# The last dense layer of a cross-attention block as seven block products, with y turned by VectorE and through DRAM

## The chip, the cores and the metric
One core of one Trainium2 chip runs the whole program. The metric is the device time of that core in microseconds. Before the change it is 2246.83 us, the median of 3 runs (2246.42 to 2249.33).

## What is computed
x and the context have 8 sequences of 256 rows and 1024 columns, in float32. The core of the reference, with the attention itself cut:

```python
x = x + attention(layernorm(x), ctx, ...)          # ends in a product with Wo, 4096 x 1024
y = layernorm(x)                                   # 2048 rows of 1024
zeros = qzeros[:, :, None] >> shifts & 15          # 4-bit zero points and weights in int32 words
w = qweight[:, None, :] >> shifts & 15             # 8 words' worth of rows: depth 1024
W = scales_full * (w - zeros_full)                 # 1024 x 1024, scales by groups of 128
x = x + y @ W + bias
```

The change touches the last two lines and the turning of y that they need. Products are made in a high and a low part of each operand: x = hi + lo, and three of the four partial products, high by high, high by low and low by high.

## The kernel before, in words
All five engines have programs written out by hand, with semaphores between them; nothing plans the order but the code. In the order of time: keys and values (to 0.16 of the span), 16 rounds of attention, the output projection (7 block products of 16 steps, numbers 0 to 111), and the last dense layer.

**The output projection** (`block_step`, lines 814 to 816) multiplies by blocks: halves of rows, of depth and of columns, in seven products instead of eight, of sums and differences of blocks. A step adds 24 matmuls of 128x512, three for each of the 8 banks of PSUM. For step s SyncE (SP) loads a left tile into `xring` and a right tile into `wraw` (`load_step`, lines 540 to 556), ScalarE makes the high parts (`step_hi`, lines 1027 and 1032), VectorE the left low part (`step_lo`, line 1339) and GpSimd the right low part (line 1634), before it a sum of right blocks (line 1646) where the product has one. `a_parts` and `b_parts` have two slots, so the parts of step s can be made when step s-2 is done. After a product VectorE adds its 8 banks to `rows` (`product_out`, line 1457); where a product goes to two places ScalarE copies it to `spare` and VectorE adds it again later (line 1464).

**The last dense layer before.** Ahead of it, within the projection's steps, VectorE unpacks the weights (`dense_full`, lines 1469 to 1474), ScalarE and VectorE make their high and low parts (lines 1101 and 1478), and from step 82 VectorE makes the statistics of the first 8 tiles of rows (line 1195) and normalizes four of them (`y_normalize`, line 1484). In the layer TensorE turns a tile of 128 rows by 8 transposes against the identity (`y_fill`, line 838), ScalarE and VectorE read the two banks as high and low part (lines 1132 and 1527), and TensorE makes two banks of 24 matmuls each (`products`, lines 241 to 243). VectorE adds each bank to its rows (line 1543), SP stores the tile (lines 603 and 607). The rest of the statistics and normalizations is done beside it; GpSimd adds the bias (line 1690). TensorE's work is 16 tiles x (8 transposes + 48 matmuls).

A part of the code as it stands, TensorE's order:

```python
for f in range(4):
    y_fill(f)
for r in range(16):
    dense(r)
    if r + 2 < 16:
        y_fill(2 * (r + 2))
        y_fill(2 * (r + 2) + 1)
```

## Time and profile before

| | us |
|---|---|
| median of 3 runs | 2246.83 (2246.42 to 2249.33) |
| span of the profiled execution | 2244.6 |
| TensorE busy | 2219.1 (99%) |
| VectorE busy | 1373.5 (61%) |
| GpSimd busy | 1392.6 (62%) |
| ScalarE busy | 1052.8 (47%) |
| granted clock of TensorE, mean | 1.000 |

The profiled execution's own time is given as its span, from the first to the last instruction; the time of a run contains also what lies around it, and the median is 2.2 us above the span. Busy time of TensorE counts overlapping matmuls once; a matmul's own 390 ns is longer than the distance between two of them, since they are pipelined. Idle time of an engine that isn't TensorE costs nothing here unless TensorE waits for it. The profile names the engines PE (TensorE), DVE (VectorE), ACT (ScalarE), POOL (GpSimd) and SP (SyncE), and L1339 is line 1339 of the kernel.

### The profile page before, as it was taken

Reading aid. Unit: us, or ns where it says so; the run is one execution under the profiler, and the core shown is the slowest. Engines: PE = TensorE matmul, PEld = TensorE weight load, DVE = VectorE, ACT = ScalarE, POOL = GpSimd, SP = SyncE. Lnnn points to the kernel's source line nnn. Section 1 sums busy time; section 2 is a strip of 40 time slices with the busy share of each in tenths; the row PEclk is TensorE's granted clock in tenths of the full one; section 3 lists DMA queues with packets and bytes.
Section 4 is the critical chain, followed back from the end, with each engine's and each line's share of the span. In section 5 each row is a group of like instructions: output and inputs, shape, how many; then the busy total and the mean of one; then the engine's idle time right before and its main releaser. Section 6 shows DMA issues by size and latency. Waiting matters only on the chain.

```text
span 2244.6 us, 33169 instructions
## 1 busy us (share of the span) xinstructions
PE 2219.1 (99%) x10562; PEld 1862.3 (83%) x10562; DVE 1373.5 (61%) x2536; ACT 1052.8 (47%) x2296; POOL 1392.6 (62%) x980
## 2 busy tenths in 40 slices
PE   8999999999999999999999999899999999999999
PEld 6888888888888888788888888778888888888887
DVE  4782575777777778877777777523675445453532
ACT  3232123767666767766666666622333333331100
POOL 1320453788888889888888888765663354454210
PEclk9999999999999999999999999999999999999999
DMA  6766675687888889887888888687654564451111
GB/s 248 269 230 217 237 269 200 204 255 242 242 260 237 245 251 271 252 262 237 242 249 248 241 250 243 205 320 259 199 187 151 162 197 151 158 193 69 47 47 47
DMA packets 299899, 476.71 MB, mean 212 GB/s; under 512 B 23568, under 2 KB 195888, under 8 KB 299824
## 3 DMA queue, kind: packets, MB, share of 16 engines
q1 hardware_dynamic: 285744, 440.12, 62.5%
q10 hardware_dynamic: 13312, 33.56, 3.8%
q0 software_dynamic: 768, 2.10, 0.3%
q8 instruction: 39, 0.64, 0.1%
q14 instruction: 36, 0.29, 0.0%
HBM read 303.70 MB, written 171.98 MB: 212 GB/s over the span
## 4 chain that ended last, share of the span: by engine, by line
PE 91%; DVE 3%; POOL 3%; DMA 1%; issue 1%; ACT 1%; SPq 0%; DVEq 0%; ACTq 0%; POOLq 0%
PE ps L241 22%; PE ps L242 22%; PE ps L243 22%; PE ps L814 9%; PE ps L815 8%; PE ps L816 8%; PE ps L838 1%; POOL rope_tmp L1561 1%; DMA left_scratch<-s_buf 0%; POOL s_buf L1561 0%; DVE rope_tmp L1170 0%; DVE rope_tmp L1171 0%; DVE rope_tmp L1169 0%; POOL wraw L1646 0%; ACT wq_t L882 0%
## 5 line engine op out<-in xcount | busy, mean ns | idle before, releaser
L241 PE MATMUL ps<-act_t,wq_t 128*128 128x512 f32 x1280 | 500.3, 391 | 1.3 <-DVE act_t L1232 0.6
L242 PE MATMUL ps<-act_t,wq_t 128*128 128x512 f32 x1280 | 499.6, 390 | 0.0
L243 PE MATMUL ps<-act_t,wq_t 128*128 128x512 f32 x1280 | 498.0, 389 | 0.0
L1634 POOL TENSOR_TENSOR b_parts<-wraw,b_parts 128x512 fp32r<-128x512 f32 x112 | 199.2, 1779 | 262.6 <-ACT b_parts L1032 262.6
L814 PE MATMUL ps<-b_parts,a_parts 128*128 128x512 f32 x896 | 349.1, 390 | 1.7 <-POOL b_parts L1634 1.4
L815 PE MATMUL ps<-b_parts,a_parts 128*128 128x512 f32 x896 | 348.6, 389 | 0.0
L816 PE MATMUL ps<-b_parts,a_parts 128*128 128x512 f32 x896 | 348.6, 389 | 0.0
L1339 DVE TENSOR_TENSOR a_parts<-xring,a_parts 128x1024 fp32r<-128x1024 f32 x112 | 147.7, 1318 | 303.7 <-ACT a_parts L1027 303.7
L1616 POOL TENSOR_TENSOR q_t<-pt_raw,q_t 128x1024 fp32r<-128x1024 f32 x124 | 302.5, 2440 | 46.3 <-ACT q_t L1010 43.5
L1561 POOL TENSOR_TENSOR rope_tmp<-rope_tmp 128x512 f32<-128x512 f32 x144 | 193.4, 1343 | 182.9 <-DVE rope_tmp L1171 182.8
L1027 ACT ACTIVATE a_parts<-xring 128x1024 fp32r<-128x1024 f32 x112 | 118.7, 1060 | 389.6 <-PE ps L816 385.5
L243 PEld LDWEIGHTS ps<-act_t,wq_t 128*128 128x128 f32 x1280 | 240.3, 188 | 51.0
L241 PEld LDWEIGHTS ps<-act_t,wq_t 128*128 128x128 f32 x1280 | 240.8, 188 | 49.9 <-DVE act_t L1232 1.8
L242 PEld LDWEIGHTS ps<-act_t,wq_t 128*128 128x128 f32 x1280 | 240.8, 188 | 45.0
L992 ACT ACTIVATE probs<-scores,neg_max 128x256 f32<-128x256 f32 x512 | 254.2, 498 | 3.6 <-DVE neg_max L1328 3.5
L1169 DVE TENSOR_TENSOR rope_tmp<-ps,rope 128x512 f32<-128x512 f32 x144 | 99.4, 690 | 218.2 <-PE ps L243 211.1
L984 ACT ACTIVATE q_t<-rope_tmp 128x512 fp32r<-128x512 f32 x128 | 81.1, 634 | 322.6 <-POOL rope_tmp L1561 322.6
L1002 ACT ACTIVATE probs<-probs,inv_sum 128x256 f32<-128x256 f32 x512 | 216.9, 495 | 2.8 <-DVE inv_sum L1335 2.6
L1610 POOL TENSOR_TENSOR q_t<-rope_tmp,q_t 128x512 fp32r<-128x512 f32 x128 | 196.8, 1537 | 5.2 <-ACT q_t L984 5.2
L814 PEld LDWEIGHTS ps<-b_parts,a_parts 128*128 128x128 f32 x896 | 168.2, 188 | 38.3 <-issue 2.6
L816 PEld LDWEIGHTS ps<-b_parts,a_parts 128*128 128x128 f32 x896 | 168.2, 188 | 34.8
L815 PEld LDWEIGHTS ps<-b_parts,a_parts 128*128 128x128 f32 x896 | 168.2, 188 | 34.7
(132 smaller groups left out, 4367.8 us busy)
## 6 DMA issues: line engine op xcount, KB each, us to landing
sq_scratch<-scores SPq DMA_DIRECT2D x124, 512.0 KB, 3.0
pt_raw<-sq_scratch SPq DMA_DIRECT2D x496, 128.0 KB, 4.0
xring<-left_scratch SPq DMA_DIRECT2D x112, 512.0 KB, 3.7
left_scratch<-s_buf SPq DMA_DIRECT2D x64, 640.0 KB, 5.2
wraw<-in_L_xattn_Wq SPq DMA_DIRECT2D x64, 512.0 KB, 4.6
wraw<-in_L_xattn_Wo SPq DMA_DIRECT2D x64, 512.0 KB, 4.5
v_scratch<-kv_t ACTq DMA_DIRECT2D x32, 512.0 KB, 3.3
k_scratch<-kv_t ACTq DMA_DIRECT2D x32, 512.0 KB, 4.8
```

The source lines that it names most:

```text
L241: eng.matmul(dst, lh, rh, start=(k == first), stop=False)
L242: eng.matmul(dst, lh, rl, start=False, stop=False)
L243: mm = eng.matmul(dst, ll, rh, start=False, stop=(k == last))
L814: pe.matmul(dst, lh, rh, start=(begins and not onto), stop=False, skip_group_check=True)
L815: pe.matmul(dst, lh, rl, start=False, stop=False, skip_group_check=True)
L816: mm = pe.matmul(dst, ll, rh, start=False, stop=ends, skip_group_check=True)
L992: e = act.activation(probs[:, par, j, qt, :], score_v[:, par, j, qt * S:(qt + 1) * S], ACT.Exp, bias=neg_max[:, par, j, qt:qt + 1], scale= ...
L1002: e = act.activation(probs[:, par, j, qt, :], probs[:, par, j, qt, :], ACT.Copy, scale=inv_sum[:, par, j, qt:qt + 1])
L1561: pool.tensor_tensor(tmp[:, 0, :], tmp[:, 0, :], tmp[:, 1, :], ALU.add).then_inc(done, 1)
L1610: pool.tensor_tensor(q_parts[:, c, j, 1, :], rope_tmp[:, 0, :], q_parts[:, c, j, 0, :].bitcast(F32), ALU.subtract).then_inc(q_lo, 1)
L1616: pool.tensor_tensor(lo, pt_raw[:, u8 % 2, :], hi.bitcast(F32), ALU.subtract).then_inc(pt_lo, 1)
L1634: pool.tensor_tensor(b_parts[:, s % 2, 1, :], wraw[s % 2][:, 0:NW], b_parts[:, s % 2, 0, :].bitcast(F32), ALU.subtract).then_inc(right_lo, 1)
```

## The change
The last layer becomes seven block products over halves of rows (even and odd tiles), depth and columns, each of 4 steps of 24 matmuls: 28 steps, numbered 112 to 139 and called D0 to D27 in the prediction. TensorE's transposes go. In their place:

- VectorE normalizes a tile and turns it in blocks of 32x32 (`turn_row`); 32 stores of 128 KB put the first 8 tiles into DRAM with the blocks in their places, issued by SP in steps 107 to 110. The other 8 tiles are normalized in D2 and D3 (four by VectorE, four by GpSimd), turned in D4 and D5, and stored by 16 DMAs on SP's queue and 16 on ScalarE's. Loads bring y back, transposed, as left tiles.
- Sums of left blocks: GpSimd makes one for each of four depths (`first_sum`), VectorE the others (`dense_sum`), a step ahead.
- The weights are no longer kept in SBUF as high and low parts: VectorE unpacks them in pairs, GpSimd makes 16 differences (`weight_sum`), SP stores them to DRAM in steps 33, 43, 51 and 62, and each step of the layer loads its right tile.
- The bias of the first 8 tiles is added in steps 93 to 110, that of the others in D4 to D7 (GpSimd) and D6 and D7 (VectorE). A product with two targets is copied to `spare` and added by GpSimd (`add_second`).
- The output is stored in 32 halves of 256 KB.

The diff, cut to its core:

```diff
-        DENSE_AT = (25, 28, 34, 37, 40, 43, 54, 57)
-
+        DENSE_AT = (25, 27, 35, 37, 43, 45, 54, 56)
+
+        SUMS_AT = (28, 38, 46, 57)
+        EVEN_AT = (91, 92, 93, 94, 95, 102, 103, 104)
+        BIAS_AT = (93, 94, 95, 96, 101, 104, 107, 110)
+        END = STEPS + 7 * KS
...
+        def store_turned(eng, tset, kt, a, done):
+            eng.dma_start(y_dram[tset, kt].rearrange("(b i) (a n) -> a i b n", b=4, a=4)[a],
+                          turned_s[32 * a:32 * a + 32, kt]).then_inc(done, 16)
...
+                if 107 <= s < 111:
+                    sp.wait_ge(y_turned, 8)
+                    for kt in (2 * (s - 107), 2 * (s - 107) + 1):
+                        for a in range(4):
+                            store_turned(sp, 0, kt, a, even_stored)
...
+                elif d == D_M6:
+                    if k == 0:
+                        dense_right(s)
+                        sp.wait_ge(y_turned, 16)
+                        for j in range(2):
+                            for kt in (j, KS + j):
+                                for a in range(4):
+                                    store_turned(sp, 1, kt, a, odd_stored[j])
+                    sp.wait_ge(odd_stored[k], 8 * 16)
+                    dense_main(s, 1, k, s - 3)
+                    sp.dma_start(left_b[:, k, :], y_dram[1, KS + k]).then_inc(b_ld[k], 16)
...
+            def dense_step(s):
+                d, k = dense_part(s)
+                pe.wait_ge(left_lo, s + 1)
+                pe.wait_ge(right_lo, s + 1)
+                onto = d in (D_M2, D_M4, D_M3)
+                for i in range(8):
+                    if k == 0:
+                        if d == D_M1:
+                            pe.wait_ge(m_out, 48 + i + 1)
+                        elif d == D_M2:
+                            pe.wait_ge(d_copied, i + 1)
+                        else:
+                            pe.wait_ge(d_out, 8 * (d - 2) + i + 1)
+                    lh, ll = [a_parts[:, s % 2, l, i * P:(i + 1) * P] for l in range(2)]
+                    rh, rl = [b_parts[:, s % 2, l, :] for l in range(2)]
+                    dst = ps[:, i, :]
+                    pe.matmul(dst, lh, rh, start=(k == 0 and not onto), stop=False, skip_group_check=True)
+                    pe.matmul(dst, lh, rl, start=False, stop=False, skip_group_check=True)
+                    mm = pe.matmul(dst, ll, rh, start=False, stop=(k == KS - 1), skip_group_check=True)
+                    if i == 7:
+                        mm.then_inc(step_done, 1)
+                    elif k == KS - 1:
+                        mm.then_inc(m_done, 1)
+
+            for s in range(STEPS, END):
+                dense_step(s)
...
+            def dense_hi(s):
+                d, k = dense_part(s)
+                act.wait_ge(step_done, s - 1)
+                act.wait_ge(right_in[s % 2], rights_in(s))
+                act.activation(b_parts[:, s % 2, 0, :], wraw[s % 2][:, 0:NW], ACT.Copy).then_inc(right_hi, 1)
+                if d == D_M1:
+                    act.wait_ge(c_ld[k], 16)
+                elif d in (D_M2, D_M4):
+                    act.wait_ge(m_ld[k], (1 if d == D_M2 else 4) * 16)
+                elif d == D_M5:
+                    act.wait_ge(s1_made, k + 1)
                 else:
-                    act.wait_ge(ffn_done, 2 * (r - 1))
-                act.activation(x2t[r % 2][:, 0, k:k + 4, :], ps[:, f % 2, :].rearrange("p (k t) -> p k t", k=4),
-                               ACT.Copy).then_inc(y_hi, 1)
-
-            for f in range(32):
-                dense_fill_hi(f)
-                if f == 11:
+                    act.wait_ge(left_summed, (0, 0, 0, KS, 0, 0, 2 * KS)[d] + k + 1)
+                act.activation(a_parts[:, s % 2, 0, :].rearrange("p (r a i) -> p a r i", r=8, a=4),
+                               dense_left(d, k).rearrange("p (a r i) -> p a r i", r=8, a=4), ACT.Copy).then_inc(left_hi, 1)
+
+            for s in range(STEPS, END):
+                dense_hi(s)
+                if s == STEPS + 2:
                     act.wait_ge(ln_var, 3)
                     act.activation(ln_tmp[:, 1, 8:16], ln_tmp[:, 0, 8:16], ACT.Sqrt).then_inc(ln_root, 1)
+                if s == STEPS + KS:
+                    act.wait_ge(m_added, 32)
+                    for i in range(8):
+                        bank_ready(act, D_M1, i)
+                        act.activation(spare[:, i, :], ps[:, i, :], ACT.Copy).then_inc(d_copied, 1)
+                if s == STEPS + KS + 2:
+                    act.wait_ge(y_turned, 16)
+                    for j in range(2, KS):
+                        for kt in (j, KS + j):
+                            for a in range(4):
+                                store_turned(act, 1, kt, a, odd_stored[j])
...
+            def turn_row(src, r):
+                dve.transpose(turned_v[:, r % 8], src.rearrange("p (k b i) -> p k b i", k=KT, b=4)).then_inc(y_turned, 1)
...
+                if s in EVEN_AT:
+                    r = EVEN_AT.index(s)
+                    if r == 0:
+                        dve.wait_ge(w_stored, 12 * 16)
+                    if r >= 4:
+                        dve.wait_ge(y_turned, r - 3)
+                    y_normalize(dve, xn[:, r % 4, :], r, y_norm)
+                    dve.wait_ge(y_norm, r + 1)
+                    turn_row(xn[:, r % 4, :], r)
+                if 102 <= s < 110:
+                    half_stats(8 + s - 102, 0)
...
+            def dense_sum(s):
+                d, k = dense_part(s)
+                if d == D_M6:
+                    dve.wait_ge(s1_made, k + 1)
+                    dve.tensor_tensor(main[k], left_b[:, k, :], left_c[:, k, :], ALU.subtract).then_inc(left_summed, 1)
+                elif d == D_M7:
+                    dve.wait_ge(m_ld[k], 3 * 16)
+                    dve.tensor_tensor(main[k], left_c[:, k, :], main[k], ALU.subtract).then_inc(left_summed, 1)
+                elif d == D_M5:
+                    dve.tensor_tensor(left_c[:, k, :], left_c[:, k, :], left_b[:, k, :], ALU.subtract).then_inc(c_less, 1)
+                elif d == D_M3:
+                    dve.wait_ge(c_less, k + 1)
+                    dve.wait_ge(m_ld[k], 5 * 16)
+                    dve.tensor_tensor(main[k], main[k], left_c[:, k, :], ALU.add).then_inc(left_summed, 1)
...
+            for s in range(STEPS, END):
+                d, k = dense_part(s)
+                if k == 1:
+                    if d == D_M1:
+                        product_out(M6)
+                    elif d > D_M2:
+                        dense_out(d - 1)
+                dense_lo(s)
+                if s + 1 < END:
+                    dense_sum(s + 1)
+                if s == STEPS + 1:
+                    for r in range(8, 16):
+                        dve.wait_ge(m_out, 48 + r - 8 + 1)
+                        half_stats(r, 1)
+                elif s == STEPS + 2:
                     inverse_std(2, 8, 8)
-                for n in range(2):
-                    dve.wait_ge(ffn_done, 2 * r + n + 1)
-                    if n == 0:
-                        dve.wait_ge(biased, r + 1)
-                    dst = rows[:, r, n * NW:(n + 1) * NW]
-                    dve.tensor_tensor(dst, ps[:, 2 + 2 * (r % 2) + n, :], dst, ALU.add).then_inc(ffn_added, 1)
-                if r + 2 < 16:
-                    dense_fill_lo(2 * (r + 2))
-                    dense_fill_lo(2 * (r + 2) + 1)
-                if r + 4 < 16:
-                    y_normalize(r + 4)
+                elif s == STEPS + 3:
+                    dve.wait_ge(even_stored, 32 * 16)
+                    for r in range(8, 12):
+                        y_normalize(dve, xn[:, r % 4, :], r, y_norm)
+                elif s == STEPS + 4:
+                    for r in range(8, 12):
+                        dve.wait_ge(y_norm, r + 1)
+                        turn_row(xn[:, r % 4, :], r)
+                elif s == STEPS + 5:
+                    for r in range(12, 16):
+                        dve.wait_ge(y_pool, r - 11)
+                        turn_row(left_b[:, r % 4, :], r)
+                elif s in (STEPS + 6, STEPS + 7):
+                    for r in (2 * (s - STEPS), 2 * (s - STEPS) + 1):
+                        dve.tensor_tensor(rows[:, r, :], rows[:, r, :], bias_rows[:, :], ALU.add).then_inc(biased_v, 1)
+            dense_out(D_M3)
...
+            def first_sum(k):
+                pool.wait_ge(m_ld[k], 2 * 16)
+                pool.wait_ge(b_ld[k], 16)
+                pool.tensor_tensor(left_b[:, k, :], left_b[:, k, :], main[k], ALU.add).then_inc(s1_made, 1)
+
+            def add_second(i, dst):
+                pool.wait_ge(d_out, 8 + i + 1)
+                pool.tensor_tensor(dst, dst, spare[:, i, :], ALU.add).then_inc(u_added, 1)
+
+            for s in range(STEPS, END):
+                d, k = dense_part(s)
+                step_lo(s)
+                if s == STEPS + 2:
+                    pool.wait_ge(ln_ready, 3)
+                    for r in range(12, 14):
+                        y_normalize(pool, left_b[:, r % 4, :], r, y_pool)
+                elif s == STEPS + 3:
+                    for r in range(14, 16):
+                        y_normalize(pool, left_b[:, r % 4, :], r, y_pool)
+                elif STEPS + 4 <= s < STEPS + 8:
+                    pool.wait_ge(y_norm, 8 + s - STEPS - 3)
+                    add_bias(8 + s - STEPS - 4)
+                elif s == STEPS + 8:
+                    first_sum(0)
+                    first_sum(1)
+                elif s in (STEPS + 9, STEPS + 10):
+                    first_sum(s - STEPS - 7)
+                elif d == D_M7:
+                    if k == 0:
+                        pool.wait_ge(biased, 12)
+                        pool.wait_ge(biased_v, 4)
+                    for i in (2 * k, 2 * k + 1):
+                        add_second(i, rows[:, ODD + i, NW:E])
```

Three places where the order of instructions changes. **VectorE, from the end of the projection's last steps into the layer**, before:

```order
L1339 TENSOR_TENSOR a_parts<-xring,a_parts 128x1024 x10
L1457 TENSOR_TENSOR rows<-ps,rows 128x512 x8
L1527 TENSOR_TENSOR a_parts<-ps,a_parts 128x512 x4
L1543 TENSOR_TENSOR rows<-ps,rows 128x512 x2
L1527 TENSOR_TENSOR a_parts<-ps,a_parts 128x512 x2
L1484 TENSOR_SCALAR dense<-rows,mean_var,inv_std 128x1024
L1195 BN_STATS stats<-rows 128x6 x6
```

and now, from the low part of D3 (`a_parts<-left_c`) on:

```order
L1639 TENSOR_TENSOR a_parts<-left_c,a_parts 128x4x8x32
L1582 TENSOR_SCALAR xn<-rows,mean_var,inv_std 128x1024 x4
L1639 TENSOR_TENSOR a_parts<-left_m,a_parts 128x4x8x32
L1587 STREAM_TRANSPOSE turned<-xn 128x8x4x32 x4
L1639 TENSOR_TENSOR a_parts<-left_m,a_parts 128x4x8x32
L1587 STREAM_TRANSPOSE turned<-left_b 128x8x4x32 x4
L1639 TENSOR_TENSOR a_parts<-xring,a_parts 128x4x8x32
L1707 TENSOR_TENSOR rows<-rows,bias_rows 128x1024 x2
L1639 TENSOR_TENSOR a_parts<-xring,a_parts 128x4x8x32
L1646 TENSOR_TENSOR left_m<-left_b,left_c 128x1024
L1707 TENSOR_TENSOR rows<-rows,bias_rows 128x1024 x2
L1639 TENSOR_TENSOR a_parts<-left_m,a_parts 128x4x8x32
```

Line 1639 is the left low part of a step, 1582 the normalization, 1587 the turn, 1707 the bias, 1646 the difference for a product's left side; `left_b` and `left_c` hold blocks of y. Four normalizations, eight turns and four bias rows now stand between the low parts, and the reads of the matmul banks come once in a product, eight at a time.

**GpSimd at the layer's start**, before (from step 110; the 16 bias rows are its whole work in the layer):

```order
L1634 TENSOR_TENSOR b_parts<-wraw,b_parts 128x512
L1646 TENSOR_TENSOR wraw<-wraw 128x512
L1634 TENSOR_TENSOR b_parts<-wraw,b_parts 128x512
L1690 TENSOR_TENSOR rows<-rows,bias_rows 128x1024 x16
```

and now, first from step 111 on, then from D7's bias row on:

```order
L1794 TENSOR_TENSOR b_parts<-wraw,b_parts 128x512 x4
L1855 ISA
L1855 TENSOR_SCALAR left_b<-rows,mean_var,inv_std 128x1024 x2
L1794 TENSOR_TENSOR b_parts<-wraw,b_parts 128x512
L1855 TENSOR_SCALAR left_b<-rows,mean_var,inv_std 128x1024 x2
L1794 TENSOR_TENSOR b_parts<-wraw,b_parts 128x512
L1852 TENSOR_TENSOR rows<-rows,bias_rows 128x1024
L1794 TENSOR_TENSOR b_parts<-wraw,b_parts 128x512
L1852 TENSOR_TENSOR rows<-rows,bias_rows 128x1024
```

```order
L1852 TENSOR_TENSOR rows<-rows,bias_rows 128x1024
L1794 TENSOR_TENSOR b_parts<-wraw,b_parts 128x512
L1878 TENSOR_TENSOR left_b<-left_b,left_m 128x1024 x2
L1794 TENSOR_TENSOR b_parts<-wraw,b_parts 128x512
L1878 TENSOR_TENSOR left_b<-left_b,xring 128x1024
L1794 TENSOR_TENSOR b_parts<-wraw,b_parts 128x512
L1878 TENSOR_TENSOR left_b<-left_b,xring 128x1024
L1794 TENSOR_TENSOR b_parts<-wraw,b_parts 128x512 x2
L1882 TENSOR_TENSOR rows<-rows,spare 128x512 x2
```

Line 1794 is the right low part of a step, 1855 the normalization (with an instruction for the library ahead of the first), 1852 the bias, 1878 the sum of left blocks. Every right low part stands behind what GpSimd does in the step before it.

**The queues that store the odd half of y**: ScalarE from the end of D6's parts to D8's right part, and SP's queue from D7's load to the loads for D9:

```order
L1216 ACTIVATE b_parts<-wraw 128x512
L1225 ACTIVATE a_parts<-xring 128x4x8x32
L332 DMA y_scratch<-turned 32x4x256 x16
L1216 ACTIVATE b_parts<-wraw 128x512
L1225 ACTIVATE a_parts<-xring 128x4x8x32
L1216 ACTIVATE b_parts<-wraw 128x512
L1225 ACTIVATE a_parts<-left_m 128x4x8x32
```

```order
L657 DMA wraw<-w_scratch 128x512
L661 DMA xring<-y_scratch 128x1024
L657 DMA wraw<-w_scratch 128x512 x2
L332 DMA y_scratch<-turned 32x4x256 x16
L661 DMA left_m<-y_scratch 128x1024
L685 DMA left_b<-y_scratch 128x1024
L661 DMA left_m<-y_scratch 128x1024
L685 DMA left_b<-y_scratch 128x1024
L657 DMA wraw<-w_scratch 128x512
```

On ScalarE, lines 1216 and 1225 are the high parts of the right and left tile of a step; 16 stores (line 332) now stand between those of D6 and D7. On SP, line 657 loads a right tile, 661 and 685 the left tiles of the third product; they stand behind the 16 stores and a wait for their landing.

## Rows read from the trace of the kernel before
**Rows 1.** The page, part 1: busy time, share of the span, instructions
```profile
PE 2219.1 (99%) x10562; PEld 1862.3 (83%) x10562; DVE 1373.5 (61%) x2536; ACT 1052.8 (47%) x2296; POOL 1392.6 (62%) x980
```
**Rows 2.** Waits of PE: for whom, us in total, times, longest us
```profile
PE ps L241 <- DVE q_t L1244: 9.2, 1, 9.2
...
PE ps L241 <- DVE q_t L1369: 2.9, 2, 2.2
...
PE ps L838 <- DVE a_parts L1527: 1.1, 1, 1.1
```
**Rows 3.** Timeline of PE at the layer's start: start, us, line, tiles, count
```profile
2051.48 1.03 PE L838 MATMUL ps<-identity,dense 128*128 128x128 f32 x8
```
**Rows 4.** Timeline of DVE at the layer's end, and of SP's queue
```profile
2236.04 0.69 DVE L1543 TENSOR_TENSOR rows<-ps,rows 128x512 f32<-128x512 f32 x1 [4.75 <-PE ps L243]
2241.48 0.69 DVE L1543 TENSOR_TENSOR rows<-ps,rows 128x512 f32<-128x512 f32 x1 [4.75 <-PE ps L243]
...
2236.76 5.77 SPq L607 DMA_DIRECT2D out<-rows  x2
```
**Rows 5.** Groups by form: line, tiles, shapes, count | busy, mean ns
```profile
L241 PE MATMUL ps<-w_parts,a_parts 128*128 128x512 f32 x256 | 100.9, 394 | 0.0
...
L838 PE MATMUL ps<-identity,dense 128*128 128x128 f32 x128 | 16.7, 272 | 1.1 <-DVE a_parts L1527 1.1
```
**Rows 6.** Timelines of ACT, DVE, POOL in one step of the output projection
```profile
2019.04 1.06 ACT L1027 ACTIVATE a_parts<-xring 128x1024 fp32r<-128x1024 f32 x1 [3.86 <-PE ps L816]
...
2020.13 1.23 DVE L1339 TENSOR_TENSOR a_parts<-xring,a_parts 128x1024 fp32r<-128x1024 f32 x1 [4.21 <-ACT a_parts L1027]
...
2020.70 1.81 POOL L1634 TENSOR_TENSOR b_parts<-wraw,b_parts 128x512 fp32r<-128x512 f32 x1 [2.38 <-ACT b_parts L1032]
```
**Rows 7.** Timelines of DVE and POOL where both work in SBUF
```profile
1579.62 2.32 DVE L1339 TENSOR_TENSOR a_parts<-xring,a_parts 128x1024 fp32r<-128x1024 f32 x1
1581.87 2.31 DVE L1478 TENSOR_TENSOR w_parts<-dense,w_parts 128x1024 fp32r<-128x1024 f32 x1
...
1579.29 1.57 POOL L1634 TENSOR_TENSOR b_parts<-wraw,b_parts 128x512 fp32r<-128x512 f32 x1 [1.93 <-ACT b_parts L1032]
1580.82 2.27 POOL L1646 TENSOR_TENSOR wraw<-wraw 128x512 f32<-128x512 f32 x1
```
**Rows 8.** Lines alone: duration ns min/median/max; last row: statistics, timeline
```profile
L1345 DVE STREAM_TRANSPOSE scores<-probs x124: 1245/1245/1249, 391.9 to 1409.1; 128x1024 f32<-128x1024 f32 x124
...
L1690 POOL TENSOR_TENSOR rows<-rows,bias_rows x16: 2366/2392/2410, 2044.2 to 2198.9; 128x1024 f32<-128x1024 f32 x16
...
L1484 DVE TENSOR_SCALAR dense<-rows,mean_var,inv_std x16: 1254/1260/2255, 1949.8 to 2197.6; 128x1024 f32<-128x1024 f32 x16
...
2081.00 3.64 DVE L1195 BATCH_NORM_STATS2 stats<-rows 128x6 f32<-128x512 f32 x6
```
**Rows 9.** Stretches (busy by engine, clock, DMA share, GB/s) and one issue by SP
```profile
1010.00:1012.00 2.00, 2.00 (x16) 1.88 (x16) 1.51 (x3) 1.86 (x4) 1.80 (x1) 1.00 0.90 244
8.00:12.00 4.00, 2.85 (x7) 2.30 (x8) 3.85 (x4) 3.35 (x4) 0.00 (x0) 1.00 1.01 404
1015.00:1016.00 1.00, 1.00 (x6) 0.84 (x5) 1.00 (x3) 1.00 (x6) 1.00 (x2) 1.00 0.97 397
...
1008.61 1.78 SPq L459 DMA_DIRECT2D pt_raw<-sq_scratch  x4
```
**Rows 10.** Timeline of DVE, the second inverse deviation, first and last
```profile
2104.52 0.73 DVE L1203 BATCH_NORM_AGGREGATE mean_var<-stats 128x2 f32<-128x12 f32 x8
...
2108.25 0.17 DVE L1217 TENSOR_TENSOR inv_std<-ln_tmp 128x8 f32<-128x8 f32 x1
```
**Rows 11.** Timeline of PE at the program's start
```profile
9.15 0.76 PE L241 MATMUL ps<-q_t,act_t 128*128 128x512 f32 x1 [9.15 <-DVE q_t L1244]
...
13.98 0.63 PE L243 MATMUL ps<-q_t,act_t 128*128 128x512 f32 x1
...
14.76 0.39 PE L242 MATMUL ps<-q_t,act_t 128*128 128x512 f32 x1
```

265 lines of the change are left out of this document (161 added, 104 removed).

## The prediction
> **What bounds the kernel now.** I read the page first: TensorE (PE) is busy 2219.1 of 2244.6 us [rows 1], so an edit pays by the matmuls it removes and costs by the gaps it opens. The chain of waits was second: TensorE's longest wait is 9.2 us at the very start; in the last layer it is one of 1.1 us [rows 2]. Third, the timeline at the edges of the last layer: the first turn of y starts at 2051.48 [rows 3], the last matmul is done at 2241.48, where VectorE (DVE) takes the last bank, and 3.1 us of add and store follow [rows 4]. So the layer takes 190.0 us of TensorE. The interval between two adds of VectorE, 5.44 us, is 24 matmuls [rows 4]: 0.2267 us each. The layer has 768 of them (3 lines x 256) and 128 turns [rows 5]: 32 x 5.44 = 174.1 us of products, and 15.9 for turns and the one wait.
>
> **What the change removes.** Seven block products of 4 steps of 24 matmuls: 28 x 5.44 = 152.3 us. With nothing to wait for, 190.0 - 152.3 = **37.7 us less**. The tail (last bank, add, store of 256 KB) stays: in the last step the banks close 0.68 us apart and VectorE's add takes 0.69.
>
> First a rule against the change. The 16 turns of a row cost VectorE 1.245 us each [rows 8], off the bound engine, but they leave 32x32 blocks that need a trip through DRAM. The Trainium skill (VectorE: DVE Perf Modes, Rules for kernel authors) says to transpose 128x128 on TensorE. By that rule the sum would be 152.3 + 14.8 (15.9 - 1.1, the trace's price of the 128 turns) = 167.1 us, with no trip. So the trip may cost 14.8 us before the rule is right; I find more.
>
> **What it adds, before the layer.** Ahead of step 112 all has cover. In a step of the output projection ScalarE (ACT) starts 0.2 us after the boundary, VectorE is done at 2.5, GpSimd (POOL) at 3.7 of 5.44 (the boundary is 2051.48 less six steps, 2018.84) [rows 6]. VectorE loses 8 low parts of the weights and gains 8 turns and 8 halves of statistics; in the densest steps (102 to 104) low part 1.23, normalization 2.25 (held up once), turn 1.25 and a statistic 0.68 make 5.4 of 5.44. GpSimd gains 16 weight differences of the size of its sums and the 8 biases moved ahead of the layer, in steps with room. SP's 8 stores a step (107 to 110) take 8 x 0.45 = 3.6 us of issue [rows 9], between its loads. Cost 0; if the cover were gone I'd expect under 2 us.
>
> **What it adds, inside.** I call the end of step 111 time 0 and the new steps D0 to D27, and followed each queue in its printed order with these durations. Two facts set the result.
> First, VectorE and GpSimd exclude each other when VectorE's operands all lie in SBUF. At 1579.62 a low part takes 2.32 instead of 1.23 us: GpSimd's instruction ran to 1580.86. Then GpSimd's takes 2.27, until VectorE's is done, and VectorE's next 2.31 [rows 7]. So they alternate. VectorE holds the port 1.15 us a row of 1024, GpSimd 1.26 for 512 and 2.37 for 1024 [rows 7, 8]; turns, statistics and reads of PSUM don't contend (all 124 turns took 1.245 to 1.249).
> Second, GpSimd's normalization of a row has no row in the trace. The nearest are its own two-operand pass over 1024, 2.39 us, and VectorE's same operation, 1.26 [rows 8]. Neither is nearer (one shares the engine, the other the operation), so I take the middle, **1.8 us**, and keep both ends: 2.4 us less or more in the sum.
>
> Step by step:
> - D1: VectorE's low part ends at 4.4, eight statistics (0.61 each) at 9.3, D2's low part at 10.4, the inverse deviation at 13.0 (the chain spans 3.9 us, 1.3 of it a wait for GpSimd [rows 10]). GpSimd's two normalizations stand ahead of D3's right low part and alternate with VectorE: it ends at 20.0, where TensorE waited since 16.3. **3.7 us.**
> - D3: VectorE makes four normalizations before D4's left low part while GpSimd makes two and D4's right part: **3.7 us**. D4 and D5: four turns each (4.7 us) ahead of a low part: **2.0 us** together. The last row is turned at 40.8.
> - ACT issues 16 of the 32 stores of the odd half of y before it may make D7's high parts: 16 x 0.47 = 7.5 us, from 40.8 to 48.3. D7's low part ends at 51.4, D6 ended at 47.4: **4.1 us**.
> - D8 needs that half back. 32 stores of 131 kB are 4.2 MB. Packets of 1 KB moved 244 GB/s at a share of 0.90 [rows 9], 270 when full: 15.5 us. The two loads that D8 needs stand behind them on SP's queue: 1.05 MB at 404 GB/s [rows 9] 2.6 us, with issue and landing some 2 more: data at 61.1. GpSimd's sum ends at 63.4, VectorE's difference at 64.6. Then two bias rows stand ahead of D8's low part on VectorE, and each of the three waits for a GpSimd instruction (second sum, D9's right part, third sum): done at 73.7. D7 ended at 56.9: **16.9 us**. D8's first bank must still be emptied, which comes after D9's difference: **1.8 us** more.
> - Later: the difference and low part ahead of VectorE's eight adds make each product's start late by 0.4 to 1.7 us: **3.8 us** in all, a third of it at D20.
> Sum of waits: 3.7 + 3.7 + 2.0 + 4.1 + 16.9 + 1.8 + 3.8 = **35.9 us**.
>
> **The clock.** At the start, after 9.15 us idle, 11 intervals take 4.83 us (0.44 each, the 1.2 GHz level) before the 0.23 of 2.4 GHz return [rows 11]: some 2.5 us lost. After gaps up to 2.2 us I see no such thing. I charge 2.5 us to the gap before D8 and none to those of 4; the ends are 0 and four times 2.5.
>
> Total: 152.3 + 35.9 + 2.5 = 190.7 us against 190.0, so 0.7 more. The profiled span is 2244.6 us; the runs' median, 2246.83, is 2.2 above it and moves alike: **2247.5 us, no measurable change**. The gain of 37.7 is real and is given back while TensorE waits for the second half of y. About 0.2% (4.5 us) is what a measurement here can tell from none.
>
> Two sentences on pages, outside the sum. The printed order has a library instruction ahead of GpSimd's first normalization; the Trainium skill (GPSIMD Engine Reference, Instruction dispatch) gives about 6 us for such a load. No run here shows it; the queues followed with 6 us give 1.8 less, since it falls into a wait and spreads GpSimd's passes.
>
> **Rivals.**
> - *The trip is short.* Stores run at the 404 GB/s of long packets (5.1 us less) and GpSimd's normalization at 1.26 (2.4 less): 2247.5 - 7.5 = **2240.0**; without the clock's loss 2237.5. For it: where SP stores 512 KB out of SBUF in the attention part, 397 GB/s are reached. Against: 244 GB/s at a share of 0.90 where four 32-partition pieces are loaded, the shape of this trip [rows 9]. Chance 0.35.
> - *TensorE drops to 1.2 GHz in each gap* (**slower**), before D3, D4, D7 and D8: 3 x 2.5 = 7.5 more: **2255.0**. It decides if a gap of 3.7 to 4.1 us is enough; the trace has only 2.2 (not) and 9.15 (yes). The Trainium skill (TensorE: Matmul & The Clock Gate) says the clock follows the engine's recent activity. Chance 0.16.
> - *The trip is long.* Two queues storing at once at 220 GB/s (3.5 more) and GpSimd at 2.4 (2.4 more): **2253.4**. Chance 0.11.
> - *All hides:* 2209. Excluded by order: the 32 stores can't begin before the last turn, which stands behind D5's low part on VectorE. It has no chance of its own.
>
> **The numbers.** Forecast 0.38 (its own range 2243 to 2252), rivals 0.35, 0.16 and 0.11: faster 0.35, same 0.38, slower 0.27. The low end is the short trip without the clock's loss and 3 us of smaller waits saved, 2234; the high end the clock's rival with GpSimd's dearer pass, 2257.
>
> **What would show it.** Right: 672 matmuls in the layer, 5.44 us a step; TensorE's waits on a_parts and b_parts of 30 to 40 us, the longest 15 to 20 before D8; ACT held some 7 us by its stores; about 20 us from the last turn to the first left_b loaded; GpSimd's normalization at 1.3 to 2.4. Wrong: a wait before D8 under 8 or over 25 us; waits before D0 to D2 or ahead of the layer; VectorE's turns held up by GpSimd; cold matmuls after the short gaps.

## The result, and the profile of the changed kernel

The changed kernel takes **2256.88 us** (median of 4 runs, 2256.16 to 2258.36), the kernel before 2247.03 beside it: ratio 1.0044, 95% interval 1.0031 to 1.0056. It is slower by 9.9 us where I had forecast no measurable change at 2247.5; the time lies at the upper end of the range (2234 to 2257), and "slower" had a chance of 0.27. The profiled execution took 2256.65 us with a span of 2254.8, 10.2 more than before.

The page, part 1, against [rows 1]: TensorE runs 224 matmuls less and is busy 23.2 us less, and still the span is longer.

```profile
PE 2195.9 (97%) x10338; PEld 1837.1 (81%) x10338; DVE 1446.3 (64%) x2572; ACT 1077.3 (48%) x2320; POOL 1527.5 (68%) x1052
```

Waits of TensorE in the layer, 2052 to 2256 us (for whom, us in total, times, longest us), where [rows 2] had one of 1.1:

```profile
PE ps L944 <- DVE rows L1675: 13.0, 2, 12.1
PE ps L944 <- POOL b_parts L1794: 8.1, 1, 8.1
PE ps L944 <- DVE a_parts L1639: 6.9, 2, 6.6
PE ps L944 <- issue: 2.4, 1, 2.4
```

and over 2010 to 2056, ahead of the layer:

```profile
PE ps L913 <- POOL b_parts L1794: 4.5, 4, 1.9
```

The timeline of TensorE gives the rest: the first matmuls of D3, D4, D7 and D8, the second of D4 and the second and third of D8 (start us, us, line, tiles, idle before and its releaser).

```profile
2082.32 0.76 PE L944 MATMUL ps<-b_parts,a_parts 128*128 128x512 f32 x1 [8.15 <-POOL b_parts L1794]
...
2093.19 0.47 PE L944 MATMUL ps<-b_parts,a_parts 128*128 128x512 f32 x1 [2.41 <-issue]
2093.50 0.39 PE L945 MATMUL ps<-b_parts,a_parts 128*128 128x512 f32 x1
...
2116.33 0.79 PE L944 MATMUL ps<-b_parts,a_parts 128*128 128x512 f32 x1 [6.57 <-DVE a_parts L1639]
...
2136.94 0.77 PE L944 MATMUL ps<-b_parts,a_parts 128*128 128x512 f32 x1 [12.08 <-DVE rows L1675]
2137.51 0.63 PE L945 MATMUL ps<-b_parts,a_parts 128*128 128x512 f32 x1
2137.93 0.63 PE L946 MATMUL ps<-b_parts,a_parts 128*128 128x512 f32 x1
```

D0 starts at 2057.69, 6.2 us later than the layer before [rows 3], and D3's gap opens three full steps behind it. The last matmul ends at 2251.60, so the layer takes 193.9 us against 190.0, and the tail 3.2. The working: 152.3 of products; start-to-start gaps beyond 0.227 of 8.3, 2.6, 6.7 and 12.2 before D3, D4, D7 and D8 (29.8); 3.0 of small waits behind D8; and 8.9 us that go nearly all to stretches in which matmuls follow each other every 0.43 us, the 1.2 GHz level. Behind each of the gaps before D3, D7 and D8 there are 13 intervals of over 0.4 us and a shorter one; what they have above 0.227 adds up to 8.5. That is 194.0. The difference to before is 6.2 + 3.9 + 0.1 = 10.2 us.

What made D8 late is in the chain of waits, cut to its longer pieces (start us, us, what):

```profile
2069.08 11.86 POOL left_b L1855 x2
2080.95 1.23 POOL b_parts L1794
2082.18 9.68 POOL left_b L1855 x2
2091.86 1.23 POOL b_parts L1794
2093.09 3.35 POOL rows L1852
...
2100.05 1.26 POOL b_parts L1794
2101.69 0.46 SPq L332
...
2117.33 5.18 DMA left_b<-y_scratch
2122.64 2.40 POOL left_b L1878
2125.07 1.23 DVE left_m L1646
2126.30 2.27 DVE rows L1707
2129.51 2.28 DVE rows L1707
2131.78 3.28 DVE a_parts L1639
2135.06 1.13 DVE left_m L1646
2136.19 0.61 DVE rows L1675
```

GpSimd works without a pause from 2069.08 to 2101.3: four normalizations of 4.8 to 6.4 us, right low parts and bias rows. SP's 16 stores stand behind the right load of D8, which waits for the last of those low parts; they take 15.1 us, while ScalarE's 16 had begun 2.8 us earlier. Then come load, sum, difference, two bias rows and D8's low part. TensorE is not in this chain from D1 to D8.

### The profile page after: what moved, and what is told of

Same layout as the page of the kernel before. It is cut to its first block, busy times and chain, and to the rows that moved or that the text cites. A ratio compares the mean times of both kernels' runs of the same rounds, so it can differ in the third digit from the quotient of the medians.

```text
span 2254.8 us, 33026 instructions
## 1 busy us (share of the span) xinstructions
PE 2195.9 (97%) x10338; PEld 1837.1 (81%) x10338; DVE 1446.3 (64%) x2572; ACT 1077.3 (48%) x2320; POOL 1527.5 (68%) x1052
## 4 chain that ended last, share of the span: by engine, by line
PE 81%; POOL 7%; DVE 5%; SPq 2%; issue 2%; ACT 1%; DMA 1%; DVEq 0%; ACTq 0%; POOLq 0%
PE ps L259 18%; PE ps L260 18%; PE ps L261 18%; PE ps L913 8%; PE ps L915 7%; PE ps L914 7%; SPq L332 1%; PE ps L944 1%; PE ps L946 1%; PE ps L945 1%; POOL b_parts L1794 1%; POOL left_b L1855 1%; POOL s_buf L1721 1%; POOL wraw L1806 1%; POOL rows L1852 1%
## 5 line engine op out<-in xcount | busy, mean ns | idle before, releaser
L1794 POOL TENSOR_TENSOR b_parts<-wraw,b_parts 128x512 fp32r<-128x512 f32 x140 | 240.5, 1718 | 266.8 <-ACT b_parts L1125 215.7
L1721 POOL TENSOR_TENSOR rope_tmp<-rope_tmp 128x512 f32<-128x512 f32 x144 | 193.3, 1343 | 181.9 <-DVE rope_tmp L1275 181.7
```

What stands on the lines that cost most here:

```text
L1721: pool.tensor_tensor(tmp[:, 0, :], tmp[:, 0, :], tmp[:, 1, :], ALU.add).then_inc(done, 1)
L1794: pool.tensor_tensor(b_parts[:, s % 2, 1, :], wraw[s % 2][:, 0:NW], b_parts[:, s % 2, 0, :].bitcast(F32), ALU.subtract).then_inc(right_lo, 1)
```

## The experiments

"The layer" below is the time from D0's first matmul to the last matmul's end, and "D8 at" is D8's start after D0's, both in the one profiled execution: they place an edit's effect, where a kernel's own executions differ by up to 8 us in their time. The ratio is to the kernel before, run beside each version, over all runs; the median of the first row is the one beside the changed kernel.

```
kernel            median    ratio, 95% interval      D0 starts  D8 at   layer
before            2247.03                            2051.48    -       190.0
after             2256.88   1.0044 (1.0031-1.0056)   2057.7     79.3    193.9
e1_act_norm       2252.31   1.0022 (1.0012-1.0031)   2059.3     75.1    189.8
e2_pool_plain     2252.41   1.0023 (1.0014-1.0032)   2059.5     75.8    190.5
e3_even_spread    2252.70   1.0025 (1.0016-1.0034)   2052.4     80.6    193.9
e4_warm_d8        2254.30   1.0032 (1.0020-1.0044)   2054.9     80.9    192.7
e5_bias_late      2253.49   1.0042 (1.0026-1.0057)   2054.8     73.1    190.2
e6_long_packets   2245.83   1.0002 (0.9993-1.0012)   2053.7     73.0    186.3
e7_pe_turn        2254.87   1.0046 (1.0031-1.0061)   2054.3     76.7    192.7
e8_pe_turn_all    2240.24   0.9976 (0.9967-0.9985)   2052.9     65.5    181.6
e9_turn_tuned     2229.34   0.9925 (0.9911-0.9938)   2052.3     53.8    169.9
e10_trip_tuned    2241.23   0.9978 (0.9969-0.9987)   2052.3     67.2    181.7
e11_trip_order    2239.75   0.9972 (0.9961-0.9984)   2051.7     68.7    183.6
e12_turn_warm     2228.34   0.9925 (0.9911-0.9938)   2051.6     55.6    171.7
```

### e1: rows 12 to 15 normalized by ACT

```diff
+                if s == STEPS + 3:
+                    act.wait_ge(shifted, 1)
+                    for r in range(12, 16):
+                        act.activation(left_b[:, r % 4, :].rearrange("p (j r) -> p j r", j=NIB),
+                                       rows[:, r, :].rearrange("p (r j) -> p j r", j=NIB), ACT.Identity,
+                                       bias=ln_tmp[:, 0, r:r + 1], scale=inv_std[:, r:r + 1]).then_inc(y_pool, 1)
...
-                    for r in range(12, 14):
-                        y_normalize(pool, left_b[:, r % 4, :], r, y_pool)
```

> Theory (price of the instruction): GpSimd's two-step normalization costs 4.8 us or more by itself, as the two at 2082.17 did (9.69 us for 2, VectorE idle for half of them). On ACT a pass over 1024 took 1.04 us, so the four rows take about 4.5, D3 and D4 wait for nothing over 1 us, the last row is turned some 10 us earlier, and D8 starts 8 to 11 us earlier: 2246 to 2249 us against 2256.9. Rival (the trip's end is set by the stores, ACT's issue and GpSimd's bias rows, not by the last turn): D3's wait goes from 8.3 to under 1, but D7 and D8 wait as much longer, and the time stays within 3 us of 2256.9.

Measured: D8 comes 4.1 us earlier after D0 and the layer is 4.1 us shorter, half of what the theory gave. D3's wait is gone, but D4 waited 2.83 for ACT, and D7's wait grew from 6.6 to 11.1 us. ACT's pass was also dearer than its copies: it reads with a stride of 8 elements. The line alone (durations in ns, min/median/max), and VectorE's normalizations, which had taken 6.89 us for four beside GpSimd's:

```profile
L1237 ACT ACTIVATE left_b<-rows,ln_tmp,inv_std x4: 2313/2375/2405, 2071.9 to 2078.8; 128x1024 f32<-128x1024 f32 x4
```
```profile
2073.41 4.85 DVE L1589 TENSOR_SCALAR xn<-rows,mean_var,inv_std 128x1024 f32<-128x1024 f32 x4
```

What follows: taking GpSimd's normalization away, with ACT's slower pass in its place, gives the layer 4 us, and not the 14 by which the four last longer than I had taken. The last turn ends at 36.9 after D0 instead of 41.0, and from there to D8 both kernels take 38.2 us. Both the theory and its rival were half right.

### e2: GpSimd's normalization without the reordering

```diff
-                eng.tensor_scalar(dst.rearrange("p (j r) -> p j r", j=NIB),
-                                  rows[:, r, :].rearrange("p (r j) -> p j r", j=NIB),
+                eng.tensor_scalar(dst, rows[:, r, :],
```

> This kernel leaves out the reordering of columns in GpSimd's four normalizations (source and target are read and written straight through). Theory A (the stride of 8 elements in the source makes it dear): each falls from 4.8 to 6.4 us to 2.4 or less, D3's wait from 8.3 to some 3 us, the time by 5 to 9 us, to about 2250. Theory B (a one-operand, two-step instruction with a scalar for each partition is dear by itself on GpSimd): 4.8 us each as before, the time within 1 us of 2256.9.

The line alone, of after and of this kernel:

```profile
L1855 POOL TENSOR_SCALAR left_b<-rows,mean_var,inv_std x4: 4811/5178/6404, 2069.1 to 2087.0; 128x1024 f32<-128x1024 f32 x4
```
```profile
L1855 POOL TENSOR_SCALAR left_b<-rows,mean_var,inv_std x4: 3775/4226/5453, 2070.9 to 2086.0; 128x1024 f32<-128x1024 f32 x4
```

The stride makes about 1 us of the 4.8 (the Trainium skill, GPSIMD Engine Reference, Performance pitfalls for Q7 kernels, gives half as much again for steps over 8 bytes; here it is a quarter), and the straight instruction still takes 3.8, against 2.39 for GpSimd's own sum of two operands of that size [rows 8]. So the price is mostly theory B's, though the time fell by 4.5 us, near theory A's 5. The layer became 3.4 us shorter for 3.9 us less on GpSimd, nearly as much as with all four passes gone in e1, where D4 waited for ACT instead. That anything beyond these microseconds would not pay is not shown, since no run takes the passes away without giving them to an engine that is then late.

### e3: the even half's stores spread out

```diff
-                if 107 <= s < 111:
+                if 107 <= s < 112:
                     sp.wait_ge(y_turned, 8)
-                    for kt in (2 * (s - 107), 2 * (s - 107) + 1):
-                        for a in range(4):
-                            store_turned(sp, 0, kt, a, even_stored)
+                    for a in range(4):
+                        store_turned(sp, 0, s - 107, a, even_stored if s < 111 else odd_stored[0])
...
+                    if k < 3:
+                        for a in range(4):
+                            store_turned(sp, 0, 5 + k, a, odd_stored[k + 1])
```

> The even half's 32 stores go four at a time, in the sequence positions 107 to 111 and D0 to D2, and not eight at a time in 107 to 110. Theory (the stores crowd SP's queue and the DMA engines, which were busy 0.96 to 1.00 of 2024 to 2048, so that the weights come late): TensorE's waits of 4.5 us between 2010 and 2052.2 fall under 1, the layer starts 4 to 6 us earlier, the time is about 2252. Rival (GpSimd's bias rows ahead of the low parts make them): those waits stay over 3 us and the time falls by under 1.5.

TensorE's waits over 2010 to 2056 in this kernel:

```profile
PE ps L916 <- POOL b_parts L1799: 0.3, 1, 0.3
```

They fell from 4.5 to 0.3 us, D0 starts at 2052.4 instead of 2057.7, and the time falls by 4.2 us: the theory, with its number. Of the 6.2 us by which D0 was late 5.3 are gone, 0.9 stay. GpSimd's bias rows stand where they stood, so they alone were not the cause. SP's queue in after shows how it came about (start us, us, line, tiles, count):

```profile
2020.74 5.29 SPq L332 DMA_DIRECT2D y_scratch<-turned  x8
...
2026.61 0.84 SPq L597 DMA_DIRECT2D wraw<-in_L_xattn_Wo  x1
2027.49 5.18 SPq L332 DMA_DIRECT2D y_scratch<-turned  x8
```
```profile
2026.15 1.29 POOL L1806 TENSOR_TENSOR wraw<-wraw 128x512 f32<-128x512 f32 x1 [2.47 <-DMA wraw<-in_L_xattn_Wo]
```

Eight stores take 5.2 us of SP (0.65 each, not the 0.45 of [rows 9]), and with its two loads SP needs 6.0 to 7.0 us for a step of 5.44; the weights come 2 us late. I had counted the issues and not the bytes: eight stores and two loads are 2.1 MB a step, 386 GB/s at 5.44 us, and the DMA engines move 323 at a share of 0.99 (stretch 2024 to 2048, busy by engine, clock, DMA share, GB/s):

```profile
2024.00:2048.00 24.00, 21.73 (x95) 17.36 (x94) 6.67 (x6) 6.14 (x7) 14.64 (x8) 1.00 0.99 323
```

In e3 four stores take 2.1 to 2.5 us of SP, and over 2015 to 2048 the engines move 309 GB/s at a share of 0.94. The edit eased SP's queue and the DMA engines together; no run parts the two.

### e4: TensorE kept at work before D8

```diff
+            WARM = {8: 48}
...
+                if s - STEPS in WARM:
+                    pe.wait_ge(zeroed, 1)
+                    z = wraw[0][:, NW:NW + P]
+                    for i in range(WARM[s - STEPS]):
+                        mm = pe.matmul(ps[:, 7, 0:P], z, z, start=False, stop=False, skip_group_check=True)
```

> 48 matmuls of 128x128 zeros (added to bank 7) fill most of TensorE's 12.2 us of waiting before D8. Theory (the wait itself brought the clock to the 1.2 GHz level: 13 intervals of 0.43 instead of 0.227, 2.9 us): D8 starts at the same distance from D0 (79.2 us) and runs at 5.5 us, the time is 2.9 us less, 2254.0. Rival (the clock falls for another reason, or the zeros do not hold it): first intervals of 0.43 as before, time within 1 us of 2256.9 or, if the zeros run over the wait, above it.

```profile
2123.82 10.21 PE L937 MATMUL ps<-wraw 128*128 128x128 f32 x90
2135.76 0.47 PE L953 MATMUL ps<-b_parts,a_parts 128*128 128x512 f32 x1 [1.73 <-DVE rows L1686]
2136.06 0.39 PE L954 MATMUL ps<-b_parts,a_parts 128*128 128x512 f32 x1
```

The zeros (each product is counted twice, and the row begins a few behind the first) end 1.7 us ahead of D8. D8 runs at the 2.4 GHz level from its first matmul. From D8's start to the end there are 111.9 us instead of 114.7: 2.8 less, as expected; D8's start was 1.6 us later in this execution, so the layer shows 1.2. The median is 2.6 us lower, but the intervals of the two ratios overlap. That the idle time before D8 brought TensorE to the lower level, and that work prevents it, is shown by the intervals of 0.23 us; its price at D8 is 2.8 us in the profiled execution.

### e5: VectorE's bias rows behind the third product's start

```diff
-                elif s in (STEPS + 6, STEPS + 7):
-                    for r in (2 * (s - STEPS), 2 * (s - STEPS) + 1):
+                elif s in (STEPS + 10, STEPS + 11):
+                    for r in (2 * (s - STEPS) - 8, 2 * (s - STEPS) - 7):
```

> VectorE's four bias rows move from D6 and D7 to D10 and D11. Theory (the queue ahead of D8's low part counts in full): that low part followed the difference 5.6 us late because of two bias rows and took 3.35 instead of 1.2 to 2.3 us; without them D8 starts 5 to 7 us earlier after D0 than 79.2 us, and the time falls by as much: 2250 to 2252. Rival (the low part then waits for GpSimd's second sum and the difference for D9 behind it): under 2.5 us are won, 2254.5 or more.

D8 comes 6.1 us earlier, as expected. Of that the layer keeps 3.7: the bias rows now take 3.46 us a pair beside GpSimd's sums, and VectorE is late in front of D11 to D13, where 0.35 us of waiting became 2.6. Over all runs the ratio is 1.0042, no different from after's 1.0044; but these are four runs, spread from 2250.0 to 2256.9, and cannot tell 3.7 us from none. The profile shows that the move is right at D8 and that a part of it comes back later, which neither line of the expectation said.

### e6: long packets

```diff
-        turned_v = turned[:, :].rearrange("p (b k r i) -> p r k b i", b=4, k=KT, r=8)
-        turned_s = turned[:, :].rearrange("p (b k n) -> p k b n", b=4, k=KT)
+        turned_v = turned[:, :].rearrange("p (k b r i) -> p r k b i", b=4, k=KT, r=8)
+        turned_s = turned[:, :].rearrange("p (k n) -> p k n", k=KT)
...
+        def store_turned(eng, tset, kt, done):
+            eng.dma_start(y_dram[tset, kt], turned_s[:, kt]).then_inc(done, 16)
+
+        def load_y(eng, dst, tset, kt, done):
+            src = y_dram[tset, kt].rearrange("(a i) (b n) -> b i a n", a=4, b=4)
+            for b in range(4):
+                eng.dma_start(dst[32 * b:32 * b + 32].rearrange("i (a n) -> i a n", a=4), src[b]).then_inc(done, 16)
```

> Each 512 KB piece of turned y is stored by one DMA of 128 partitions with 4 KB runs in DRAM (8 issues a half instead of 32), and the loads back are four DMAs of 128 KB each. Theory A (the 1 KB pieces and the 32 issues make the stores slow, 4.2 MB in 15.1 us): the odd half is stored in some 10.5 us, ACT is held under 4 us instead of 13 so that D7 waits under 2 us instead of 6.7, the waits ahead of the layer fall to half, loading takes 1.3 us more; the time falls by 5 to 8 us, to about 2250. Theory B (bytes alone set it, or the loads' pieces give it back): the same 14 to 16 us, the time within 2 us of 2256.9.

The largest gain of a single edit to the changed kernel: 11 us, to the level of the kernel before. Stretches of this kernel (busy by engine, clock, DMA share, GB/s), two during the stores and one during the loads back:

```profile
2101.00:2104.00 3.00, 3.00 (x15) 2.50 (x14) 3.00 (x2) 1.58 (x2) 2.18 (x3) 1.00 1.03 406
2104.00:2107.00 3.00, 3.00 (x15) 2.36 (x13) 3.00 (x2) 0.00 (x0) 3.00 (x1) 1.00 1.03 421
2113.00:2116.00 3.00, 1.23 (x6) 0.69 (x4) 0.00 (x0) 0.00 (x0) 1.42 (x1) 1.00 1.14 215
```

and the stores of after:

```profile
2101.00:2116.00 15.00, 8.76 (x39) 6.93 (x37) 7.03 (x4) 2.10 (x3) 5.72 (x4) 0.87 0.95 253
```

ACT's four stores take 2.9 us instead of 14 (16 at 0.89), so D7's wait falls from 6.6 to 1.2; the waits ahead of the layer fall to 1.8, and D8 comes 6.3 us earlier. The price stands in the third row: loads that gather 1 KB pieces move 215 GB/s with the DMA engines full. The slowness was moved from the stores to the loads, of which only the first pair is on the path. The Trainium skill (DMA: Bandwidth & Descriptors, Specifications) names 512 B as the smallest transfer for line rate; by that, pieces of 1 KB should be long enough, and in this trip they moved 215 to 253 GB/s beside 406 to 421 for 4 KB. But every DMA of 1 KB pieces here covers 32 partitions and 128 KB, and every store of 4 KB runs 128 partitions and 512 KB: what of the difference the length of the piece makes is not shown, since the edit changed all three and the number of issues together.

### e7 and e8: the odd half turned by TensorE

```diff
+                if s == STEPS + D_M6 * KS:
+                    pe.wait_ge(y_norm, 12)
+                    pe.wait_ge(y_pool, 4)
+                    for f in range(16):
+                        kt, g = FILLS[f]
+                        if f < 8:
+                            pe.wait_ge(d_out, f + 1)
+                        else:
+                            pe.wait_ge(y_copied, f - 7)
+                        for i in range(4):
+                            src = left_b[:, i, kt * P:(kt + 1) * P] if g else xn[:, i, kt * P:(kt + 1) * P]
+                            mm = pe.transpose(ps[:, f % 8, i * P:(i + 1) * P], src, identity[:, :])
+                        mm.then_inc(y_filled, 1)
```

The 16 fills are copied into `turned` by ACT (12) and VectorE (4), and stay there: the third, fourth and fifth product (`D_M6`, `D_M7` and `D_M4`) read them in SBUF. Both have e5's edit too. e8 adds the edit of e3, and VectorE normalizes rows 12 to 15 in place of GpSimd:

```diff
+                elif s in (STEPS + 4, STEPS + 5):
+                    for r in (2 * (s - STEPS) + 4, 2 * (s - STEPS) + 5):
+                        y_normalize(dve, left_b[:, r % 4, :], r, y_norm)
```

> The odd half of y is turned by TensorE, 64 turns of 128x128 through PSUM between D7 and D8, copied out by ACT and VectorE, and never goes through DRAM; the bias rows stand at D10 and D11. The GpSimd normalizations stay. Theory (after the last turn the trip costs 38.2 us in after, of which TensorE can work on only 8 to 17; on TensorE the turn costs 7.4 us of work and about 5 of waiting for the first sum, difference and parts): D7 follows D6 at once, D8 starts 12 to 14 us after D7's end instead of 12.2 plus D7's 6.7, and no stretch of 0.43 us intervals stands at D7 or D8: the time falls by 9 to 13 us, to 2244 to 2248. Rival (emptying 8 banks, filling and copying them 16 times is itself longer than the trip): D8 starts over 20 us after D7's end and the time is 2252 or more.

> As the turn on TensorE, with the even half's stores spread over 107 to D2 and all odd rows normalized by VectorE (D3 to D5) instead of GpSimd. If the terms add (waits ahead of the layer 4.5 us, D3's and D4's waits 11, cold stretch at D3 2.9, the trip 9 to 13), the layer takes 152.3 + 13 + 3 = 168 us from D0 at 2052.4, and the time is 2225, some 22 us under the kernel before. Rival (a wait moves: VectorE's queue with four more normalizations, or the stores' traffic in D0 to D2, holds D3 to D7): 2232 or more.

e7 failed its expectation: D8 comes only 2.5 us earlier, and the ratio, 1.0046, is that of after. D7 no longer waits, but GpSimd's normalizations still hold D3 for 8.2 us and D4 for 3.5, and the 12.1 us of waiting before D8 have become 7.2 of turns and a wait of 10.7. e8 is the first version that is faster than the kernel before, by 0.24%, but at 2240.2, not 2225. What the 10.7 us are, in e7 and e8 alike, the timelines of e8 between D7 and D8 say, TensorE, GpSimd and VectorE:

```profile
2100.50 3.65 PE L963 MATMUL ps<-identity,left_b 128*128 128x128 f32 x32
2103.99 3.66 PE L963 MATMUL ps<-identity,xn 128*128 128x128 f32 x32
2118.37 0.76 PE L944 MATMUL ps<-b_parts,a_parts 128*128 128x512 f32 x1 [10.72 <-DVE a_parts L1657]
```
```profile
2108.88 1.26 POOL L1813 TENSOR_TENSOR b_parts<-wraw,b_parts 128x512 fp32r<-128x512 f32 x1 [14.96 <-ACT b_parts L1230]
2110.09 4.63 POOL L1897 TENSOR_TENSOR left_b<-turned 128x1024 f32<-128x1024 f32 x2
```
```profile
2112.47 3.34 DVE L1664 TENSOR_TENSOR left_m<-left_b,left_c 128x1024 f32<-128x1024 f32 x1 [4.53 <-POOL left_b L1897]
```

The turns take 7.2 us, as priced. The 10.7 are a queue: ACT makes D8's right high part only after its 12 copies, GpSimd's first sum stands behind the right low part that needs it, and VectorE's difference then waits for the port until GpSimd's second sum is done (3.34 us instead of 1.23).

### e9: that queue cut

ACT makes D8's right high part ahead of the copies, VectorE makes the first sums, and ACT normalizes rows 12 to 15 one at a time in D2, D4, D5 and D6:

```diff
+                if s == STEPS + D_M6 * KS:
+                    dense_hi_right(s)
...
+                if s == STEPS + 7:
+                    dense_out(D_M2)
+                    copy_fill(8)
+                    first_sum(0)
+                if STEPS + 8 <= s < STEPS + 11:
+                    first_sum(s - STEPS - 7)
```

> The turn on TensorE again, with what its trace showed in the way: the right high part of D8 is made before the copies out of PSUM and not behind them, the four first sums are VectorE's and not GpSimd's, rows 12 to 15 are normalized by ACT in D2, D4, D5 and D6, and VectorE's bias rows stand at D9 and D10. Theory (the 17.6 us between D7's end and D8 in e8 are 7.2 of turns and a queue of 10 that can be cut to 3): D8 starts 54 to 57 us after D0 (65.5 in e8), D3 to D7 wait under 1.5 us together (4.0 in e8), the time is 2226 to 2230. Rival (the copies out of PSUM and the port shared by VectorE and GpSimd keep D8 over 62 us after D0): 2236 or more.

2229.34 us, 0.75% faster than the kernel before (interval 0.62% to 0.89%), inside the expectation; D8, at 53.8, comes a little ahead of the 54 to 57 expected. The waits of TensorE from 2052 on:

```profile
PE ps L945 <- issue: 3.2, 1, 3.2
PE ps L945 <- DVE a_parts L1669: 1.6, 2, 1.1
PE ps L945 <- DVE rows L1713: 0.9, 1, 0.9
PE ps L945 <- DVE spare L1713: 0.7, 1, 0.7
```

The layer takes 169.9 us: 152.3 of products, 7.2 of turns, and 10.4 of waits and low clock.

### e10 and e11: the trip given the same care

e10 is e6 with the even half spread, the normalizations on VectorE (8 to 13) and ACT (14, 15), and the bias rows at D9 and D10; SP stores ahead of D8's right load, which comes behind the first loads of y. e11 puts that load between the stores and the loads of y; against the changed kernel, where it stood ahead of the stores, this reads:

```diff
                     if k == 0:
-                        dense_right(s)
                         sp.wait_ge(y_turned, 16)
                         for j in range(2):
                             for kt in (j, KS + j):
                                 store_turned(sp, 1, kt, odd_stored[j])
+                        dense_right(s)
```

> The trip through DRAM kept and given the same care: stores of 512 KB with 4 KB runs, the even half's spread over 107 to D2, rows 8 to 13 normalized by VectorE and 14 and 15 by ACT, SP's stores ahead of D8's right load, VectorE's bias rows at D9 and D10. Theory (the trip after the last turn was 31.9 us in e6 and falls by 6 for the bias rows and 2 for SP's queue, the last turn comes 5 us earlier): D8 starts 57 to 61 us after D0, with a stretch of 0.43 us intervals behind it, the time is 2230 to 2236: the trip costs more than the turn on TensorE, but its excess of 38 us was mostly of this kernel's making. Rival (the DMA engines, at a share of 1.0, set the trip and not the queues): D8 over 66 us after D0 and 2240 or more.

> As the tuned trip, with D8's right load issued behind SP's stores but ahead of the eight loads of y, and not behind those of the first pair. Theory (in the tuned trip the first sum began at 2109.66 because it stands behind GpSimd's right low part of D8, whose load was issued at 2101.1 and landed at 2107.6; the left data were there earlier): the first sum begins 2 to 5 us earlier, and the time is 2236 to 2239. Rival (the loads of y in 1 KB pieces, 210 to 240 GB/s at a share over 1.0, are the bound): the first sum waits for left_b instead and the time stays within 1 us of 2241.2.

e10's rival holds: D8 at 67.2, 2241.2 us. In e10 the first sum stood behind GpSimd's low part, whose weights had been loaded late; e11 removes that and the first sum waits for the data themselves:

```profile
2105.22 1.26 POOL L1810 TENSOR_TENSOR b_parts<-wraw,b_parts 128x512 fp32r<-128x512 f32 x1 [5.89 <-ACT b_parts L1221]
2109.26 2.34 POOL L1894 TENSOR_TENSOR left_b<-left_b,left_m 128x1024 f32<-128x1024 f32 x1 [2.78 <-DMA left_b<-y_scratch]
```

The stores of e11 were issued from 2089.99 on; 19.3 us later the first pair is back. From 2093 on the DMA engines stand at a share of 1.01 to 1.14, first at 401 GB/s, and at 213 over the last 5 us, when nothing but the loads is left. e11 is 1.5 us below e10, but the intervals of the two ratios overlap, so no difference is shown. With this layout the DMA engines set the trip, and the turn on TensorE is 10 us better. A layout with long pieces both ways was not tried.

### e12: the last gap filled

```diff
+                    for i in range(13):
+                        pe.matmul(ps[:, 0, 0:P], z, z, start=False, stop=False, skip_group_check=True)
```

> As the tuned turn on TensorE, with 13 products of 128x128 zeros (onto bank 0, which D8 then starts afresh) in the 3.2 us between the last turn and D8. Theory (that idle time put TensorE at the 1.2 GHz level for 8 intervals, 1.6 us): D8 starts as before and runs at 0.227 us an interval, the time is 2227.5 to 2228. Rival (the level depends on more than the last 3 us): intervals of 0.43 stay, time within 0.5 us of 2229.3.

D8 ran at 0.23 us an interval, as the theory said, and it won nothing that can be measured (both ratios 0.9925): from D8 to the end there are 116.1 us here and 116.0 in e9. (That D8 itself stands 1.8 us later comes from a wait of 1.5 us for VectorE at D3 in this execution.) D10 and D11, which VectorE feeds with a sum, a difference and a low part each, waited 1.0 and 1.2 us, where in e9 only D11 did, 1.1. TensorE's slow stretch had been cover for VectorE.

## What of the prediction held and what failed, point by point

The change was forecast to make no difference and made the kernel 9.9 us slower. Two steps of the prediction failed. The work ahead of the layer, put at nothing, cost 6.2 us; and GpSimd's normalization and the stores of y were priced too low. That the time, 2256.88, still lies inside the range, 0.1 us below its end, is luck: that end was added up from other causes, three more losses of the clock and a pass of 2.4 us.

- **Layer without waits, 152.3 us, and the tail: right.** The matmuls follow at 0.227 us, 24 to a step, 224 fewer in all.
- **"Ahead of step 112 all has cover ... Cost 0; if the cover were gone I'd expect under 2 us": wrong, 6.2 us, two thirds of the miss of 9.4.** The step counted SP's issues (8 x 0.45 = 3.6) and not the bytes of the stores and loads together: 386 GB/s were asked for, and 323 moved. The eight issues took 5.2. e3 spread the stores and brought D0 back to 2052.4.
- **GpSimd's normalization, 1.8 us, ends 1.26 and 2.39: wrong, 4.8 alone and up to 6.4 beside VectorE.** Both bounds came from two-operand GpSimd work or from VectorE, and the price lay outside them. D3 waited 8.3 instead of 3.7. It cost less than its size: e1 shows 4.1 us for the layer. The last turn ended at 41.0 after D0, forecast 40.8, but by luck: D4 started at 35.5 instead of some 29, and while TensorE waited VectorE had got its first four turns behind it, so that the waits of 2.0 us for the turns did not come.
- **VectorE and GpSimd alternate: right** in every pair seen (3.35 for a low part or difference beside GpSimd's sum). The library load: a configuration row of some nanoseconds stands in the trace, none of 6 us.
- **D7, 4.1 us: 6.7.** ACT's 16 stores took 14 us at 0.89 each, not 7.5 at 0.47 ([rows 9] has 0.45, of a load). With both queues storing, the DMA engines stood at a share of 0.95, and SP's last two stores, when ACT's were done, took 0.45 again.
- **The trip before D8.** Forecast: last turn 40.8, data at 61.1, first sum done 63.4, low part 73.7, D8 at 75.7. Measured: 41.0, 64.9, 67.4, 77.4, 79.3. The forecast had 15.5 us for all 32 stores; from the last turn to the end of the last issue it took 18.1, of which 3.0 passed before SP's first store, behind a load that waited for GpSimd (2098.7 to 2101.7), and 15.1 over its 16. ACT was storing in those 3.0 us, with the engines at a share of 0.74, so how much of the 2.6 us missed is that wait and how much a rate of 253 GB/s instead of 270 stays open. Loading took 5.8 us instead of 4.8, and the chain behind the data 14.3 instead of 14.6. The rival of the long trip had the nearest account of this part, 3.5 us more for the stores.
- **The clock: right for what I charged** (2.5 at D8, measured 2.8). TensorE fell to the lower level before D3 and D7 too, as the rival had it, not before D4. But those 5.7 us lie inside the 79.3 that GpSimd and the stores set, as the chain shows, so the rival's 7.5 more was wrong for another reason than its condition. The granted clock agrees with the Trainium skill (TensorE: Matmul & The Clock Gate, Part 1: The HAM clock gate): it follows the engine's recent activity, as e4 shows with work put into the wait before D8.
- **Later waits, 3.8 us: 3.0.**

The sum: 6.2 ahead, 3.6 up to D8, 0.4 less behind it: 9.4 over the forecast. Two of the signs of being wrong that it had named came, waits ahead of the layer and slow matmuls behind gaps other than D8's. Its seven waits add up to 36.0 and were given as 35.9, which changes nothing.

**The rule against the change.** The Trainium skill (VectorE: DVE Perf Modes, Rules for kernel authors) has 128x128 transposes on TensorE; by it I had worked out 167.1 us for the layer. e9, with only the odd half turned there, takes 169.9, and the trip at its best here 181.7: the rule agrees with the runs. But e7 shows that following it alone gains nothing; e8 and e9 differ only in the order of the queues around the turn, in the place of the bias rows and in who does the passes, and that is 11 us.

## What to carry to other kernels

When a change puts stores into a stretch that already loads, count the bytes of a step against what the engines move there, not only the issues: past that point each issue grows longer, and everything behind it on the queue is late. A pass that has no row must be bounded on the engine that runs it, and for an unseen kind of instruction well beyond the nearest kind's price. And an operation moved off the bound engine is worth only what its way back takes: here the wait for it was 38 us long, of which TensorE had 16 us of work to cover it with.

## What was not expected of the hardware

- GpSimd's subtract-and-multiply with a scalar for each partition takes 3.8 us for 128x1024 read straight, 4.8 with a stride of 8 elements, where its sum of two operands takes 2.39. ACT's pass with the same stride takes 2.3 to 2.4 where its copy takes 1.04; VectorE's takes 1.26 with the stride.
- The issue of a 128 KB store took 0.45 us when nothing else stored, 0.65 in a run of eight on one queue with the DMA engines full, and 0.89 to 0.94 with two queues storing.
- In stretches mostly of stores with 4 KB runs the DMA engines moved 406 to 421 GB/s, with stores of 1 KB runs 253, with loads that gather 1 KB pieces 215. The 1 KB DMAs cover 32 partitions each, the 4 KB stores 128.
- TensorE's level after a wait (intervals of over 0.4 us): 2.41 us idle before D4 in after, none; 3.4 before D4 in e3, 7; 4.13 before D5 in e10, 12. But in e1 eight followed on 1.93 us of idle time before D5, 7.7 us after D4 had waited 2.83 and shown none. So the length of the last gap alone does not tell it.
- The fall can come after TensorE has gone back to work. In e9 D8 starts at the 2.4 GHz level, 3.16 us after the last turn, and 1.45 us later the intervals become 0.43 us for eight matmuls (rows below); the granted clock is 1.00 from 2106.0 to 2107.5 and 0.51 from there to 2111.0.

```profile
2106.10 0.47 PE L945 MATMUL ps<-b_parts,a_parts 128*128 128x512 f32 x1 [3.16 <-issue]
...
2107.32 0.42 PE L947 MATMUL ps<-b_parts,a_parts 128*128 128x512 f32 x1
2107.55 0.62 PE L945 MATMUL ps<-b_parts,a_parts 128*128 128x512 f32 x1
```
